# A Perceiver layer on one core: loads held back at the start, the two weighted sums of a pair side by side, self-attention computed turned

## What is computed

```python
# 1: cross-attention (H = 16, D = 64)
q = (layernorm(lat) @ Wq); k, v = split(layernorm(ctx) @ Wkv)
attn = softmax(clip(q @ k.T * D ** -0.5, -11.0, 11.0))      # 16 x 128 x 12544
x = x + (attn @ v).reshape(n, H * D) @ Wo + bo
# 2: self-attention over the 128 rows (16 heads of 16, LoRA added to each weight)
attn = softmax(Q @ K.T / sqrt(16)); x = x + lora_linear(attn @ V, Wo, bo, Ao, Bo)
# 3: linear layer with inputs and weights rounded to fp8
x = x + (fp8(h / x_scale) * x_scale) @ (weight * weight_scale).T + bias
```

## Time and profile before

| | |
|---|---|
| median of 3 runs | 1068.35 us (1067.48 to 1068.49) |
| profiled execution, its own time | 1069.03 us |
| its span in the profile | 1067.3 us |
| PE busy | 1059.9 us (99%) |
| PE weight loads busy | 901.8 us (85%) |
| DVE busy | 933.8 us (87%) |
| ACT busy | 663.2 us (62%) |
| mean granted TensorE clock | 0.999 of full speed |

### The profile page before, as it was taken

The page is one execution under the profiler, slowest core; times in us unless marked ns, Lnnn a source line. Parts: engine busy times, 40 slices in busy tenths (PEclk is TensorE's granted clock), DMA queues, the critical chain, the costliest instruction groups (busy, mean ns, idle before and its releaser), DMA issues.

```text
span 1067.3 us, 18064 instructions
## 1 busy us (share of the span) xinstructions
PE 1059.9 (99%) x5501; PEld 901.8 (85%) x5501; DVE 933.8 (87%) x1329; ACT 663.2 (62%) x934; POOL 177.5 (17%) x213
## 2 busy tenths in 40 slices
PE   9999999999999999999999999999999999999998
PEld 7888888888888888888888888888888888888886
DVE  4999999999999999988898888888888888878885
ACT  4666666666666666656666666666666666665642
POOL 3233332332332333322000000000000000000000
PEclk9999999999999999999999999999999999999999
DMA  5312212212212212122151111111111111111000
GB/s 202 95 55 70 74 51 72 74 49 74 74 49 74 64 59 74 52 81 69 53 117 37 44 31 43 44 30 44 44 30 44 38 35 44 31 44 31 1 1 6
DMA packets 52925, 58.78 MB, mean 55 GB/s; under 512 B 31202, under 2 KB 33316, under 8 KB 52772
## 3 DMA queue, kind: packets, MB, share of 16 engines
q1 hardware_dynamic: 52468, 58.19, 18.3%
q10 hardware_dynamic: 432, 0.27, 0.1%
HBM read 58.20 MB, written 0.13 MB: 55 GB/s over the span
## 4 chain that ended last, share of the span: by engine, by line
PE 98%; DMA 1%; DVE 0%; SPq 0%; issue 0%; ACT 0%; DVEq 0%
PE wide L464 25%; PE wide L465 25%; PE wide L466 25%; PE wide L505 18%; DMA wq<-in_Wq_dram 1%; PE wide L527 1%; PE wide L541 1%; PE wide L556 1%; PE wide L562 0%; PE wide L549 0%; PE wide L522 0%; PE wide L764 0%; PE wide L534 0%; PE wide L515 0%; PE wide L747 0%; PE wide L694 0%
## 5 line engine op out<-in xcount | busy, mean ns | idle before, releaser
L836 ACT ACTIVATE ex<-wide,c_rstd 128x512 f32<-128x512 f32 x392 | 270.5, 690 | 221.9 <-PE wide L466 214.0
L464 PE MATMUL wide<-qk_hi,d_hi 128*128 128x512 f32 x784 | 310.8, 396 | 0.0
L465 PE MATMUL wide<-qk_lo,d_hi 128*128 128x512 f32 x784 | 307.4, 392 | 0.0
L466 PE MATMUL wide<-qk_hi,d_lo 128*128 128x512 f32 x784 | 305.3, 389 | 0.0
L1050 DVE TENSOR_TENSOR ph<-ex,ph 128x1024 fp32r<-128x1024 f32 x195 | 237.9, 1220 | 15.8 <-ACT ph L843 15.8
L1059 DVE TENSOR_TENSOR den_all<-den_all,ex 128x1024 f32<-128x1024 f32 x193 | 236.3, 1225 | 4.7
L505 PEld LDWEIGHTS wide<-ph,vhl 128*128 128x128 f32 x1568 | 213.8, 190 | 15.2
L505 PE MATMUL wide<-ph,vhl 128*128 128x256 f32 x1568 | 218.7, 282 | 0.0
L829 ACT ACTIVATE vhl<-wide,c_rstd 128x512 fp32r<-128x512 f32 x196 | 135.1, 689 | 131.2 <-PE wide L466 131.2
L843 ACT CAST ph<-ex 128x1024 fp32r<-128x1024 f32 x195 | 204.1, 1046 | 0.1
L1023 DVE TENSOR_SCALAR ex<-ex 128x1024 f32<-128x1024 f32 x195 | 135.3, 694 | 73.0 <-ACT ex L836 68.3
(11 more groups left out here) (163 smaller groups left out, 615.5 us busy)
## 6 DMA issues: line engine op xcount, KB each, us to landing
t_all<-in_ctxT_dram SPq DMA_DIRECT2D x98, 384.0 KB, 3.1
x_pair<-in_ctx_dram SPq DMA_DIRECT2D x49, 256.0 KB, 2.7
diff<-sig_all SPq DMA_DIRECT2D x194, 0.5 KB, 1.9
wkv<-in_Wo_dram SPq DMA_DIRECT2D x2, 1024.0 KB, 9.9
wq<-in_Wq_dram SPq DMA_DIRECT2D x2, 512.0 KB, 8.7
wkv<-in_Wv_dram SPq DMA_DIRECT2D x2, 512.0 KB, 6.8
wkv<-in_Wk_dram SPq DMA_DIRECT2D x1, 512.0 KB, 10.5
wkv<-in_Wk_dram SPq DMA_DIRECT2D x1, 256.0 KB, 3.2
```

What stands on the lines that cost most here:

```text
L464: pe.matmul(dst, hi, mhi, start=start, stop=False)
L465: pe.matmul(dst, hi, mlo, start=False, stop=False)
L466: return pe.matmul(dst, lo, mhi, start=False, stop=stop)
L836: act.activation(ex[b][:, c * HC:(c + 1) * HC, :], sc_bank[c][:, :].rearrange("p (h q) -> p h q", h=HC), ACT.Exp, scale=c_rstd[s4][:, b:b ...
```

## The change

There are three parts, and a move.

1. **Head.** SP waits for `s_wkc` and `s_xin[0]` before it issues pair 1, and for the first half of `Wq` before it issues the second half and everything behind it.
2. **Loop.** Both weighted sums of a pair are computed behind the scores and values of both tiles, sixteen matmuls in a row. The last pair of pass 1 stays as it was.
3. **Self-attention.** All exponentials are computed head by head and write their sum too (`accum_out`, into `a_sum`). The roles in the product are swapped: values are the stationary operand (32 columns: a head's 16 and 16 zeros, so that two heads add up side by side) and transposed probabilities the moving one, so the output is already transposed. The reciprocals are spread over 256 columns by DVE (`a_spread`), transposed by two matmuls and copied by ACT (`a_scale`); one DVE multiplication gives `aoT`. The two transposes, the copy, and three `full_rows` are gone.
4. **Move.** `fp8_weights` on DVE goes from behind the probability copies to just behind `hT`.

```diff
             sp.dma_start(t_pair[0], ctxT[0, :, :, :]).then_inc(s_tin[0], 16)
+            sp.wait_ge(s_wkc, 16)
+            sp.wait_ge(s_xin[0], 16)
             load_rows(1, 1)
             load_columns(1, 1)
+            sp.wait_ge(s_wq[0], 16)
             sp.dma_start(wq[:, 1, :, :], Wq[:, 1, :, :]).then_inc(s_wq[1], 16)
...
-                    weighted_sum(gp, b, first, last, saved=p * MH if first else 0, ended=ended)
+                    final = p == PASSES - 1 and static and i == PAIRS - 1
+                    begins = static and i == 0
+                    if final:
+                        weighted_sum(gp, b, False, last, ended=ended)
+                    elif b == 1:
+                        weighted_sum(gp, 0, begins, False, saved=p * MH if begins else 0)
+                        weighted_sum(gp, 1, False, last)
...
             transposed_probs(2)
-            full_rows(bank[3], 1)
+            def weighted_values(n):
+                for k in range(KD):
+                    for a in range(2):
+                        ins = pe.matmul(bank[5][32 * n:32 * n + 32, k * P:(k + 1) * P],
+                                        av[:, 4 * k + n, a:a + 2, :].rearrange("p c d -> p (c d)"),
+                                        a_pT[:, 4 * n + 2 * k + a, :], start=(k == 0 and a == 0), stop=(k == KD - 1 and a == 1))
+                ins.then_inc(s_apv, 1)
+            weighted_values(0)
             transposed_probs(3)
-            for at in range(AH):
-                ins = pe.matmul(bank[5][:, at * (AD + 1):(at + AW) * (AD + 1)], a_pT[:, at, :],
-                                av[:, h:h + AW, :].rearrange("p h v -> p (h v)"), start=True, stop=True)
+            weighted_values(1)
+            for k in range(KD):
+                ins = pe.matmul(bank[4][:, k * P:(k + 1) * P], a_spread[:, k, :], ident[:, :], start=True, stop=True)
+            weighted_values(3)
+            weighted_values(2)
             pe.matmul(bank[6][:, 0:D], ones_row[:, :], abo_row[:, :], start=True, stop=False)
-            full_rows(bank[7], 1)
-            pe.wait_ge(s_ao, 1)
-            for k in range(KD):
-                ins = pe.transpose(bank[4][:, k * P:(k + 1) * P],
...
-                    ins = act.activation(a_p[:, heads, :], a_p[:, heads, :], ACT.Exp, scale=AD ** -0.5)
+                    for at in range(4 * n, 4 * n + 4):
+                        ins = act.activation(a_p[:, at, :], a_p[:, at, :], ACT.Exp, scale=AD ** -0.5,
+                                             accum_out=a_sum[:, at:at + 1])
...
+            dve.wait_ge(s_apv, 4)
+            dve.wait_ge(s_scale, 1)
+            dve.tensor_tensor(aoT[:, :, :], bank[5][:, 0:D].rearrange("p (k q) -> p k q", k=KD), a_scale[:, :, :], ALU.mult)\
+               .then_inc(s_aoT, 1)
```

More of the change, by code:

```diff
@@ L52, in perceiver_layer @@
     HT = P // AD
-    AW = 7
     assert N == P and D == 2 * P and ctx.shape[1:] == (P, 2, D)
@@ L130, in perceiver_layer @@
         a_recip = sb("a_recip", [P, AH])
+        a_sum = sb("a_sum", [P, AH])
         amax = sb("amax", [P, 1])
@@ L154, in perceiver_layer @@
         hT, aqT, aoT = latT, qT[:, 0:KD, :], qT[:, KD:2 * KD, :]
-        ao = wkE[:, 0, :].rearrange("p (h d) -> p h d", h=AH)
+        a_spread, a_scale = (wkE[:, n, :].rearrange("p (k q) -> p k q", k=KD) for n in range(2))
         s_x = sem("x_loaded")
@@ L233, in perceiver_layer @@
         s_apTp = sem("self_probs_transposed")
-        s_apT = sem("self_probsT_banks_0_1_3_ready")
-        s_apT2 = sem("self_probsT_bank_2_ready")
+        s_apT = sem("self_probsT_banks_0_1_2_ready")
+        s_apT2 = sem("self_probsT_bank_3_ready")
         s_apv = sem("self_outputs_computed")
-        s_ao = sem("self_outputs_normalised")
-        s_aoTp = sem("self_outputs_transposed")
+        s_scale = sem("reciprocals_ready")
+        s_spread = sem("reciprocals_spread")
+        s_scalep = sem("reciprocals_turned")
         s_aoT = sem("self_outputsT_ready")
@@ L623, in pair @@
                     next_p = p + 1 if static and i == PAIRS - 1 and b == 1 else p
-                    first = static and i == 0 and b == 0
                     last = static and i == PAIRS - 1 and b == 1
@@ L962, in _ @@
             act.wait_ge(s_const, 5)
-            act.copy(av[:, 0:AH, 0:AD], bank[1][:, 0:D].rearrange("p (h d) -> p h d", h=AH)).then_inc(s_av, 1)
+            act.copy(av[:, :, 0:3:2, :], bank[1][:, 0:D].rearrange("p (m a d) -> p m a d", a=2, d=AD)).then_inc(s_av, 1)
             for n in range(1, 4):
                 self_exp(n)
-            act.wait_ge(s_apTp, 3)
-            act.copy(a_pT[:, 8:12, :], bank[2][:, :].rearrange("p (h t) -> p h t", h=4)).then_inc(s_apT2, 1)
+            act.wait_ge(s_apTp, 4)
+            act.copy(a_pT[:, 12:16, :], bank[3][:, :].rearrange("p (h t) -> p h t", h=4)).then_inc(s_apT2, 1)
+            act.wait_ge(s_scalep, 1)
+            act.copy(a_scale[:, :, :], bank[4][:, 0:D].rearrange("p (k q) -> p k q", k=KD)).then_inc(s_scale, 1)
             act.wait_ge(s_fqTp, 1)
@@ L1249, in _ @@
             dve.tensor_copy(hT[:, :, :], bank[4][:, 0:D].rearrange("p (k q) -> p k q", k=KD)).then_inc(s_hT, 1)
+            fp8_weights()
             dve.wait_ge(s_const, 4)
@@ L1268, in _ @@
                                       ALU.subtract).then_inc(s_ashift, 1)
-            for n in (0, 1, 3):
+            for n in range(3):
+                if n == 2:
+                    dve.wait_ge(s_aexp, 4)
+                    link(dve.reciprocal(a_recip[:, :], a_sum[:, :]))
+                    for k in range(KD):
+                        ins = dve.tensor_copy(a_spread[:, k, :].rearrange("p (n a d) -> p n a d", n=4, a=2),
+                                              a_recip[:, :].rearrange("p (n k a) -> p k n a", k=KD, a=2)[:, k, :, :].unsqueeze(3)
+                                              .to_broadcast([P, 4, 2, AD]))
+                    ins.then_inc(s_spread, 1)
                 dve.wait_ge(s_apTp, n + 1)
```

35 lines of the change are left out of this document (10 added, 25 removed).

## The result

The changed kernel takes 1070.73 us (median of 15 runs) beside 1068.64 for the kernel before: a ratio of 1.0025 (1.0019 to 1.0032). The ratio goes by means, the medians alone are 0.20% apart: four of the 15 executions, at a mean granted clock of 0.997 or 0.998 where the others had 0.999 or more, took 1072.55 to 1073.31 us. One of the 15 of the kernel before, 2149.46 us, is left out of the means. The forecast was 1065.8, with a range up to 1068.9.

What follows compares the result with a forecast made beforehand. PE, with 98% of the chain that ended last, was taken as the bound. Gains of 1.6 (loop), 0.7 (head) and 0.3 (self-attention), 2.6 us, off a median of 1068.35 gave 1065.8; range 1064.2 to 1068.9 for 8 in 10.

Steps and rivals of the forecast that it cites:

- The loop's gain: Loop on PE: joining a pair's two weighted sums (a merge) saves 0.018 us net, 1.6 us over 89 pairs.
- debt: Rival, loop: the 0.025 us behind a weighted sum grows with its length, -0.6 instead of +1.6, 1068.0; chance 0.10.
- I take 0 for this wait: Loop, pass 0: next pair's first-tile values waiting for DVE's `v_low` cost 0; upper bound 0.03 us in some 46 pairs.
- the values wait: Rival, loop, pass 0: DVE's chain is longer, every pair waits for `v_low`; at 0.13 us a pair 1071.8; chance 0.12.
- The head: Start of the kernel: holding transfers lets queries start earlier; gain between nothing and 1.5 us, taken as 0.7.
- the landing of the second half: Head: second half of `Wq`, issued at about 10.5, lands at 12.5 to 14, before PE wants it; cost nothing.
- The fallback price: Head: if the second half of `Wq` is not covered, each microsecond of its delay past 14.5 is paid.
- order: Rival, head: the held transfers never overtook, `Wq` was late for another reason; head gives 0, 1066.5; chance 0.16.
- Self-attention: Self-attention: output product at 1057.2 instead of 1057.46, 0.3 us gained, with four exponentials at 1.38 us, each sum 0.06.
- `fp8_weights` at nothing: Self-attention: its 2.1 us on DVE move into a gap of 2.22 us where DVE waits for PE, costing nothing.
- The sum: Whole kernel: loop 1.6, head 0.7 and self-attention 0.3 make 2.6 us gained.

Runs made afterwards that it cites:

- s1_attn_only: The kernel before with only the turned self-attention and the moved `fp8_weights`: 1068.55 us, ratio 1.0000 (0.9991 to 1.0009).

## Why the prediction was wrong, step by step

**The loop's gain, "0.025 - 0.007 = 0.018 us" a merge.** Right: 0.020 us a pair in pass 1, and in pass 0 too once the wait is gone. No debt grows with the row.

**"I take 0 for this wait."** This step failed, in two ways. For the usual pair of pass 0 the working found a margin of 0.05 us, and a stall of 0.03 as its bound; measured is 10.1216 - 10.1003 = 0.02 us a pair, 0.9 over the pass. The stall that I worked out is not there: `clip` did start 0.03 us after the exponential, as I argued, and the values start on time. What I put at nothing without a reason is that the matmuls behind a wait that is only just met run slower, 1.379 us for six instead of 1.360. That the loss stays within my bound of 0.03 is luck. Graver: I worked the wait out in one usual pair only. The pairs where DVE's chain is longer than usual (the first, the one behind the value folds, the one behind the turn) were counted for what they do to the return to 512 columns, not for `v_low`. They cost 0.5, 1.1 and 0.3 us. The rival "the values wait" had the mechanism, but put its price, 0.13 us, on every pair: it was 0.02 in the usual one and 1.9 us in three. I gave it 0.12.

**The head.** Its first half was right and even undersized: the queries start at 9.4 to 9.6 in all five profiled kernels with the first wait on pair 1 and the second half of `Wq` behind it, and at 10.35 to 11.08, mean 10.62, in the eight whose head is that of before. The profiled execution of before was the latest of these, which one trace could not tell me. The step that failed is the landing of the second half: "at 2 to 3.5 us of latency and data it lands at 12.5 to 14". I took the load's short path from no row; it took 6.17 us, and landed at 15.77. PE wanted it at 13.75, earlier than the 14.5 that I had, since the queries came earlier. The fallback price, "each microsecond of its delay past 14.5 is paid", was the case that came true: the value fold at 21.4 with both waits against 20.29 is +1.1 us, where -0.7 was predicted. Two smaller slips: six loads stand behind the second half of `Wq`, not seven, and the loads ahead of the wait were slowed before 8 us already, which I had ruled out: by then 1.39 MB had moved in all in the kernel before, and 1.58 MB in the changed kernel, where nothing else was on its way.

**The rival "order"** is refuted: a load that stands ahead of others in SP's list is slowed by them. Issued at 3.27, the first half has landed at 10.35 to 11.08 with everything behind it, at 10.9 with the columns of pair 0 and the second half behind it, and at 9.4 to 9.6 with only the columns and, from 7.4 us on, pair 1. The bytes agree: by 9.4 us the kernel before has moved 1.84 MB, which is all that stands ahead of the held loads, and the changed kernel 1.87; yet the first half landed at 11.04 in one and at 9.59 in the other, so part of the 1.84 MB were held loads. The Trainium skill ("DMA: Bandwidth & Descriptors", section "Queues, rings and completion order") says that each engine consumes its descriptors in ring order, but also that a later one may finish its write before an earlier one. The runs contradict neither. What they rule out is the step from ring order to a whole transfer, that the held loads could not have mattered: it is wrong by 1.1 us.

**Self-attention.** The pace was right (1.38 us for four exponentials, as worked out), though by two errors that cancel: up to the next instruction they take 1.02 without sums, not 1.14, and a sum costs 0.09, not 0.06. The rest was lost on PE. In `s1_attn_only`:

```profile
1051.25 0.66 PE L747 MATMUL wide<-ident,wq 128*128 128x128 f32 x4
1051.83 1.06 PE L762 MATMUL wide<-t_all,av 128*32 128x128 f32 x8
1052.83 0.66 PE L747 MATMUL wide<-ident,wq 128*128 128x128 f32 x4
```

From the third transposes to the output product it is 1057.13 - 1051.25 = 5.88 us, where I had 5.6 (1051.6 to 1057.2): transposes 0.58 us instead of 0.5, a quarter of the products 0.99 instead of 0.89, the reciprocals 0.64 instead of 0.45, and only the last half is shorter, 1.46 instead of 1.8. The third transposes also start 0.19 us behind the exponentials of their bank, where I had 0.07. So +0.1 instead of -0.3. `fp8_weights` at nothing: right.

**The sum.** -2.6 predicted. Measured by parts: the row's gain -1.8, its waits +0.9 in the usual pairs of pass 0 and +1.9 in three pairs, head +1.1, self-attention +0.1. That is +2.2, and 1070.73 - 1068.64 = 2.09.

## What to carry to other kernels

- When work is moved away from between a producer and its consumer, work out the consumer's wait in every place where the chain of the producer's engine is longer than usual (first and last iterations, turns, iterations with extra work), not only in the steady state: there up to the whole 0.95 us that was moved became a wait (1.0 us at the largest place, 0.5 and 0.3 at the other two).
- In an in-order list, put what another engine waits for ahead of what nobody waits for soon. Here that was worth little in the old order (a rest of -0.4 us) and 2.9 us in the new one (from +1.0 to -1.9).
- A load that is held must be costed from the measured time of a load in that stretch, from issue to landing. A hold moves a wait; here it moved it from the first half to the second and made it longer.

## What was not expected of the hardware

- A load is slowed by loads issued behind it: the first half of `Wq` by 1.1 us in the mean, the second by 1.1 (6.17 against 5.05, one execution each).
- A sum output is an instruction of its own on ACT (`ACTIVATION_READ_ACCUMULATOR`, 0.19 to 0.24 us in the profile, overlapping the next exponential) and costs 0.09 us of ACT's time each.
- A stall costs more than its row names: 0.80 us is named at 491.93, the starts lose 0.96, and the six matmuls behind it another 0.13.
- Products with 32 stationary columns overlap where two groups for different output partitions follow each other. In `s1_attn_only` eight alone take 1054.40 - 1053.41 = 0.99 us, sixteen in two groups 1056.50 - 1055.04 = 1.46. By the starts of single matmuls each group keeps its 0.109 us from one to the next, but the second group begins 0.47 us behind the first, and for a while starts of the two stand 0.03 us apart. Why it begins only behind the fifth matmul of the first group, no run here tells:

```profile
1053.41 1.06 PE L762 MATMUL wide<-t_all,av 128*32 128x128 f32 x8
1054.40 0.71 PE L775 MATMUL wide<-ident,wkE 128*128 128x128 f32 x4
...
1055.04 1.53 PE L762 MATMUL wide<-t_all,av 128*32 128x128 f32 x16
1056.50 0.69 PE L781 MATMUL wide<-abo_row,ones_row 1*128 1x256 f32 x2
```

- A hold in the head goes with more executions at a slightly lower clock. In the six kernels with a hold 12 of 70 executions have a mean granted clock of 0.997 or 0.998, in those with the head of before 8 of 175; they take about 2 us more than the others of their kernel. None of them was profiled, so where in the execution the clock was lower, and whether PE's idle time in the head is the cause, is not shown.
